# Moving the token loads to a second DMA queue, and the key bias' sums behind the features

## The reference, cut to what matters

```python
x = _ln(tgt + sa, g1, be1)
q1 = x @ wq.T + bq
k2 = memory @ wk.T + bk
cscores = jnp.einsum('btd,bmd->btm', q1, k2) / jnp.sqrt(jnp.float32(DKQ))
ca = jnp.einsum('btm,bmd->btd', jax.nn.softmax(cscores, axis=-1), v2)
```

## Time and profile before

| | us |
|---|---|
| median of three runs | 532.81 (532.42 to 533.29) |
| the profiled execution | 532.86 |
| its span | 531.1 |
| PE busy | 519.0, 98% |
| DVE busy | 325.7, 61% |
| ACT busy | 222.0, 42% |
| POOL busy | 104.1, 20% |

### The profile page before, as it was taken

How to read it: one execution, slowest core, us unless ns; L and a number is a source line. 1 busy time by engine, 2 the same in 40 slices (tenths; PEclk the granted TensorE clock), 3 DMA queues, 4 the chain that set the end, 5 groups by cost and what they waited for, 6 DMA issues and landing times.

```text
span 531.1 us, 7541 instructions
## 1 busy us (share of the span) xinstructions
PE 519.0 (98%) x3014; PEld 496.3 (93%) x3014; DVE 325.7 (61%) x556; ACT 222.0 (42%) x388; POOL 104.1 (20%) x93
## 2 busy tenths in 40 slices
PE   8899999999999999999999999999999999999996
PEld 6799999789988878999999999999999899999996
DVE  3753789895698986877365544277674354442225
ACT  2853542483589865264535153206413231320200
POOL 2430430022032135054006200005530000000000
PEclk9999999999999999999999999999999999999999
DMA  8941212031589961228022222002220033100004
GB/s 231 349 166 57 64 73 79 1 113 56 192 287 325 305 224 34 79 97 227 1 79 80 80 80 79 1 0 81 80 79 1 0 123 117 53 28 0 1 1 123
DMA packets 18428, 53.75 MB, mean 101 GB/s; under 512 B 1625, under 2 KB 2425, under 8 KB 15833
## 3 DMA queue, kind: packets, MB, share of 16 engines
q1 hardware_dynamic: 18332, 53.20, 30.6%
q10 hardware_dynamic: 60, 0.07, 0.1%
HBM read 51.63 MB, written 1.64 MB: 100 GB/s over the span
## 4 chain that ended last, share of the span: by engine, by line
PE 81%; DVE 11%; DMA 3%; ACT 3%; issue 2%; SPq 0%; POOL 0%; DVEq 0%; ACTq 0%
PE ps L576 21%; PE ps L578 21%; PE ps L577 21%; PE ps L611 3%; DMA tok<-x_in 2%; PE ps L589 2%; DVE cnL L1179 2%; PE ps L750 1%; DMA cnR<-ctxn_in 1%; PE ps L752 1%; PE ps L751 1%; PE ps L622 1%; PE ps L724 1%; PE ps L726 1%; PE ps L725 1%
## 5 line engine op out<-in xcount | busy, mean ns | idle before, releaser
L576 PE MATMUL ps<-XH,WH 128*128 128x400 f32 x352 | 122.5, 348 | 0.9 <-DVE AL L1191 0.4
L578 PE MATMUL ps<-XH,WL 128*128 128x400 f32 x352 | 121.5, 345 | 0.0
L577 PE MATMUL ps<-XL,WH 128*128 128x400 f32 x352 | 121.4, 345 | 0.0
L576 PE MATMUL ps<-AH,WH 128*128 128x400 f32 x288 | 100.2, 348 | 0.6 <-DVE AL L1195 0.2
L578 PE MATMUL ps<-AH,WL 128*128 128x400 f32 x288 | 99.4, 345 | 0.0
L577 PE MATMUL ps<-AL,WH 128*128 128x400 f32 x288 | 99.3, 345 | 0.0
L576 PEld LDWEIGHTS ps<-XH,WH 128*128 128x128 f32 x352 | 66.1, 188 | 2.7 <-DVE AL L1191 0.8
L577 PEld LDWEIGHTS ps<-XL,WH 128*128 128x128 f32 x352 | 66.2, 188 | 0.1
L578 PEld LDWEIGHTS ps<-XH,WL 128*128 128x128 f32 x352 | 66.2, 188 | 0.0
L488 POOL TENSOR_TENSOR WL<-WR,WH 128x512 fp32r<-128x512 f32 x38 | 52.4, 1409 | 67.2 <-ACT WH L904 67.2
L576 PEld LDWEIGHTS ps<-AH,WH 128*128 128x128 f32 x288 | 54.1, 188 | 2.1 <-DVE AL L1195 1.9
(11 more groups left out here) (181 smaller groups left out, 817.8 us busy)
## 6 DMA issues: line engine op xcount, KB each, us to landing
WR<-wts_in SPq DMA_DIRECT2D x19, 1024.0 KB, 4.8
ctR<-ctxt_in SPq DMA_DIRECT2D x16, 722.0 KB, 5.0
cnR<-ctxn_in SPq DMA_DIRECT2D x16, 512.0 KB, 5.2
cnR<-ctxn_in SPq DMA_DIRECT2D x8, 256.0 KB
tok<-x_in SPq DMA_DIRECT2D x4, 384.0 KB, 10.4
tok<-x_in SPq DMA_DIRECT2D x1, 1536.0 KB
cnR<-ctxn_in SPq DMA_DIRECT2D x8, 160.0 KB
VR<-wvo_in SPq DMA_DIRECT2D x4, 256.0 KB, 6.2
```

Of the source, the lines that this page charges most:

```text
L576: pe.matmul(dst, wh, half(mh, h, k), start=(k == 0), stop=False)
L577: pe.matmul(dst, wh, half(ml, h, k), start=False, stop=False)
L578: mm = pe.matmul(dst, wl, half(mh, h, k), start=False, stop=(k == KC - 1))
```

## The change

Loads: SP keeps the weights and constants, in their order. ACT issues the loads of x: the first half's three DMAs are its first instructions, the second half's three stand behind its split of VR and OR piece 1.

Key bias: `key_product` reads the transposed, not yet scaled tokens from PSUM and multiplies with `keyG` = key · g1. The part of be1 goes into the constant: the sum over bq · bk + key · be1, made in `key_constants`, four instructions on 128x4 elements; the old reduction for that constant goes. The products of half 0 stand behind the features of half 0 and before the statistics of half 1; those of half 1 among the evacuations of `U_A`. As the tokens' PSUM banks are then read longer, `to_tokens(1, 1)` waits for the first half's key products and `cross_scores(0)` for the second's. PE runs `combine_cross(1)` before `to_tokens(1, 1)` instead of behind it.

```diff
-            load_x_tail(0)
-            load_x(0)
-            load_x(1)
             load_vo(2)
             load_vo(3)
...
-            load_x_tail(1)
-            load_x(2)
-            load_x(3)
             sp.dma_start(cst[:, :], consts).then_inc(consts_loaded, 16)
...
                         elif h == 1:
                             pe.wait_ge(x_ready, 8 * i + j + 1)
+                            if i == 1:
+                                pe.wait_ge(key_ready, 1)
...
                 if b == 0:
                     pe.wait_ge(x_ready, 16)
+                    pe.wait_ge(key_ready, 2)
...
             combine_cross(0)
+            combine_cross(1)
             to_tokens(1, 1, U_VO, XS)
-            combine_cross(1)
             combine_cross(2)
...
+            def load_x(h):
+
+                bs = slice(HB * h, HB * (h + 1))
+                act.dma_start(tok[TA:T, bs, :], x[bs, TA:T].rearrange("b t d -> t b d")).then_inc(x_tail[h], 16)
+                for i in (2 * h, 2 * h + 1):
+                    act.dma_start(tok[0:TA, 2 * i:2 * i + 2, :],
+                                  x[2 * i:2 * i + 2, 0:TA].rearrange("b t d -> t b d")).then_inc(x_loaded[i], 16)
+
+            load_x(0)
             for k in range(KC):
                 split_vo(k)
+                if k == 1:
+                    load_x(1)
...
-                    if i == 1:
-                        key_product(h, k)
...
             def key_product(h, k):
 
-                key = gv[:, KC + k:KC + k + 1]
+                src, key = ps[:, 4 + k, 0:HALF], keyG[:, k:k + 1]
...
+            def key_constants():
+
+                key = gv[:, KC:2 * KC]
+                dve.wait_ge(gv_ready, 1)
+                dve.tensor_tensor(keyG[:, :], key, cst[:, C_G1:C_G1 + KC], ALU.mult)
+                settle(dve.tensor_tensor(key, key, cst[:, C_E1:C_E1 + KC], ALU.mult))
+                settle(dve.tensor_tensor(qk[:, :], qk[:, :], key, ALU.add))
+                settle(dve.tensor_reduce(qks[:, 0:1], qk[:, :], AX.X, ALU.add))
...
             key_vector(1, 1)
+            key_constants()
             unit(U_VO, 1, [2])
...
             norm_features(1, 0, [3])
+            for k in range(KC):
+                key_product(0, k)
             statistics(1, HB)
...
-            unit(U_A, 0)
+            unit(U_A, 0, [0, 1])
+            key_product(1, 0)
+            key_product(1, 1)
+            unit(U_A, 0, [2])
+            key_product(1, 2)
+            unit(U_A, 0, [3])
+            key_product(1, 3)
```

More of the change, by code:

```diff
@@ L196, in build @@
         qks = small("qks", [P, 1])
+        keyG = small("keyG", [P, KC])
         ones1 = small("ones1", [P, 1])
@@ L267, in build @@
         u_o_ready, u_q_ready, u_k_ready = sem("u_o_ready"), sem("u_q_ready"), sem("u_k_ready")
-        qks_ready = sem("qks_ready")
         gv_made, gv_ready = sem("gv_made"), sem("gv_ready")
@@ L350, in _ @@
         def _(sp):
[L351 to L358, removed]
             def load_vo(k):
@@ L1289, in key_product @@
             def key_product(h, k):
-                key = gv[:, KC + k:KC + k + 1]
+                src, key = ps[:, 4 + k, 0:HALF], keyG[:, k:k + 1]
                 if k == 0:
[L1293 to L1296, removed]
+                    dve.tensor_scalar(keyX[h][:, :], src, key, qks[:, 0:1], ALU.mult, ALU.add).then_inc(key_step, 1)
                     return
                 dve.wait_ge(key_step, (KC - 1) * h + k)
-                dve.scalar_tensor_tensor(out=keyX[h][:, :], in0=half(XT, h, k), scalar=key, in1=keyX[h][:, :],
+                dve.scalar_tensor_tensor(out=keyX[h][:, :], in0=src, scalar=key, in1=keyX[h][:, :],
                                          op0=ALU.mult, op1=ALU.add
                                          ).then_inc(key_step if k < KC - 1 else key_ready, 1)
+            def key_constants():
[5 more added lines that the diff above has]
+                settle(dve.tensor_reduce(qks[:, 0:1], qk[:, :], AX.X, ALU.add))
             def self_max(h):
@@ L1462, in _ @@
             settle(dve.tensor_tensor(qk[:, :], cst[:, C_CBQ:C_CBQ + KC], cst[:, C_CBK:C_CBK + KC], ALU.mult))
-            dve.tensor_reduce(qks[:, 0:1], qk[:, :], AX.X, ALU.add).then_inc(qks_ready, 1)
             self_max(0)
```

## The result

The changed kernel takes 535.88 us (median of 4 runs, 534.88 to 536.48), against 532.76 us before in the same comparison; the ratio is 1.0061 (95% interval 1.0048 to 1.0074). It is slower by 3.1 us; 534.9 had been forecast. The profiled execution took 535.65 us, with a span of 533.9. The clock in tenths stays at 9 all through the page of before; after it reads

What follows compares the result with a forecast made beforehand. PE, busy for 519.0 of 531.1 us, was taken as the bound, so only its waits could change. From 532.86 us, +1.4 (start) and +1.3 - 0.65 (middle) gave 534.9 us, range 532.0 to 536.3.

Steps and rivals of the forecast that it cites:

- What bounds it: Whole kernel: PE is busy 519.0 of 531.1 us, matmuls stay unchanged, so only PE's idle time and new waits can change.
- The loads, +1.4: Start: x on a second queue delays VR/OR piece 1 to 10.8 us, so statistics end at 14.7 against 13.3; +1.4 us.
- XS, -1.15: Middle, combine_cross(0): moved key products free DVE, XS chunk 3 comes sooner and PE's 1.03 us wait goes; -1.15 us.
- The token chain: Middle: transposes behind combine_cross(1) make tokens and the weight product's low parts late, so U_A waits; +1.3 us, -1.15 included.
- What comes back, -0.65: Middle, U_A's second half: DVE ends half 1's features earlier, the 0.43 us wait and some 0.2 refill go; -0.65 us.
- The sum: Whole kernel: +1.4 in the start and +1.3 - 0.65 in the middle make +2.05, so 534.9 us.
- my own forecast: Whole kernel: the time lies between 533.9 and 535.8 us; chance 48%.
- the slow end: Rival: even queue sharing costs +2.1 us in the start, key constants or products are late by 0.7; 536.3 us; 10%.
- Two free queues: Rival, start: the two queues cost nothing or help, start -0.8, middle +0.65; 532.7 us; 25%.
- The faster one: Rival: start gains 0.8 to 1.5 us and a shorter token chain gives no new wait at U_A; 531.0 us; 13%.
- Moved products that do not free DVE: Rival, middle: high parts hold DVE anyway, so -1.15 is not had and transposes are later still; 536.0 us; 4%.

Runs made afterwards that it cites:

- run 3: Kernel before with all loads of x on ACT's queue, and DVE taking x's first statistics ahead of the low part of VR/OR piece 1; ratio to before 1.0036.
- run 2: Changed kernel with all loads back on SP, so only the key bias' part and the new PE order; ratio to before 1.0039.
- run 4: Changed kernel with all loads back on SP, plus three useless matmuls on PE behind the last transpose of to_features(1,1); ratio to before 1.0027.
- runs 1: Kernel before with only the loads moved, x on ACT's queue and the rest on SP's; ratio to before 1.0038.
- 9: Kernel before with only the three loads of x's first half on ACT's queue; ratio to before 1.0024.
- run 7: Changed kernel with loads back on SP, and two DVE context splits and one of ACT moved behind U_A's first half; ratio to before 0.9989.
- run 6: Changed kernel with all loads back on SP and combine_cross(1) behind to_tokens(1,1) again; ratio to before 1.0022.

## Why the prediction was right, point by point

- **What bounds it.** Right: matmuls unchanged, all of the difference in PE's waits and clock.
- **The loads, +1.4.** Right in mechanism: piece 1 was put at 10.8 and came at 10.81, and DVE's list holds the statistics behind its low part. That x is complete before piece 1 shows in run 3 alone (10.97 against 11.16). Measured 1.09 in the pair of profiles, 1.3 to 2.0 by the runs, 1.7 between the means of profiles. That 10.81 hit 10.8 so closely is luck: the four profiles with two queues have 10.5, 10.8, 11.2 and 11.9. The Trainium skill ("DMA: Bandwidth & Descriptors", on queues and rings) states that each DMA engine goes round-robin over the queues it has work for. By my estimate of even sharing piece 1 would come last, near 11.5; the four values lie on both sides of that, and run 3 has it last.
- **XS, -1.15.** Right: the wait of 1.03 is gone, the fourth group starts 2.21 us behind the first instead of 3.28 (-1.07), `key_constants` ran inside the idle time and left 0.25 us of it.
- **The token chain, +1.3 at U_A, the -1.15 included.** Right in place and size: waits of 1.18 (forecast 1.3) for tokens and 1.33 for low parts. The start of `U_A` lies 17.24 us behind that of `combine_cross(0)`, before 15.72: +1.5.
- **What comes back, -0.65.** Right that the wait of 0.43 goes; the key products were hidden. From the start of `U_A` to `cross_scores(0)` it is 12.38 us instead of 11.86, and 0.75 less than before without the clock's 1.27. No low part of half 1 was long, but POOL's split began only behind them, so this trace does not test what stretches them; the key products, which now read one input from PSUM, took 0.69 and 0.63 beside it, where one with both inputs in SBUF took 1.67 before.
- **The term that was missing.** I priced both waits as time only. The clock fell to 0.50 behind them and took 1.2 to 1.3 us more in the changed kernel, 1.45 in run 2 (against run 4). The middle was forecast at +0.65 and measured +2.04: +1.52, -0.75 and +1.27.
- **The sum.** In the profiles: first unit +1.09, from there to `combine_cross(0)` +0.12, middle +2.04, all that follows -0.45, together +2.8, the difference of the spans. The last is mostly a shorter wait for `ptL` in the cross attention (0.4 against 0.8 us), which differs between profiles of one kernel too (0.8 and 1.7 us in the two of before). That the sum came so near to +2.05 is in part luck: the clock's 1.27 was missing, and a start 0.3 cheaper than forecast and 0.3 us that no term had took half of it back.
- **The rivals.** The median, 535.88, lies just above the 533.9 to 535.8 that I gave my own forecast, and nearer to the 536.3 of the slow end than to 534.9. But the slow end's terms did not come: the start cost 1.1 in the pair of profiles and 1.7 between the means, not 2.1, and neither the key constants nor the key products were late. Two free queues: refuted by runs 1 and 9. The faster one: refuted by run 2; run 7 shows that its condition, no new wait at U_A, needs the splits moved. Moved products that do not free DVE: refuted by the profile.

## What to carry to other kernels

A wait that is removed gives time only if the next meeting of the engines has room: here 1.46 us of slack between tokens and PE was all that held the chain, and reordering PE to cover a wait of 2.24 us used it up. Look at what stands in the lists of the other engines between the late result and its reader, and move what is not yet needed behind it; here that took 3.04 us off the middle of run 2, the clock's part included, more than the edit itself had cost. A load on another queue came earlier here only at the price of what it shares the DMA engines with (x complete at 10.97 instead of 11.97, piece 1 at 11.16 instead of 8.58), so ask first which of the two is waited for. Short waits that follow each other may cost more than their sum, so look at the granted clock behind them, and in more than one execution.

## What the runs showed of the hardware that I had not expected

- Two waits of 1.18 and 1.33 us within 4.2 us were followed by a granted clock of 0.50 for about 3 us, in both profiles that had them (the changed kernel and run 2); the mean clock was at 0.997 or below in eight of the nine executions. With 0.84 us of matmuls in the second wait, of which 0.65 us was left, it stayed at 1.00 (run 4; none of eight executions at 0.997 or below).
- The same wait does not always do it. In the start, a wait of 2.15 us (one of 1.02 ahead of it) was followed by the lower level in run 3, while 1.50 and 2.10 us in run 9, and 2.28 us in run 7, were not. In the middle, one of 2.24 us was not in the profile of run 6, but five of its twelve executions had a low mean clock. What decides stays open. All that PE does between the two waits of the changed kernel is transposes, and the wait of run 6 stands ahead of transposes too; whether that matters for the clock no run tests, since run 4 filled the wait with other matmuls.
- With two queues loading, the DMA engines' share stayed at 0.88 to 1.07 (the changed kernel, 2 to 15 us), while piece 1 came 2.2 us later and piece 2 about 1 us sooner (12.14 instead of 13.10).
